# Second attention in runs of four and eight units, and gate inputs scaled once per event

## Reference

```python
x = _layernorm(x + _L0_attn_ref(x, ...))      # 16 heads of 8, decay by distance
x = _layernorm(x + _L0_ffn_ref(x, ...))       # one of 8 experts per token
x = _layernorm(x + _L1_attn_ref(x, ...))      # 16 heads of 64, below
x = _layernorm(x + _L1_ffn_ref(x, ...))       # 128 -> 512 -> 512 -> 512 -> 128
```

```python
q = _rmsnorm((x @ Wq).reshape(B, T, H, D), q_rms_w)
k = _rmsnorm((x @ Wk).reshape(B, T, H, D), k_rms_w)
v = (x @ Wv).reshape(B, T, H, D)
gate_logits = jnp.einsum('bthd,hd->bht', k, u_n) / math.sqrt(D)
gate = jax.nn.softplus(gate_logits)
bias = -dist[None, None] * omega_eff[None, :, None, None] * gate[:, :, None, :]
scores = jnp.einsum('bihd,bjhd->bhij', q, k) * scale + bias      # causal
y = jnp.einsum('bhij,bjhd->bihd', softmax(scores), v)
```

## Time and profile before

| | us |
|---|---|
| three runs | 2251.53, 2245.86, 2246.51 |
| median | 2246.51 |
| the profiled execution, its own time | 2246.59 |
| its span in the trace | 2244.8 |

### The profile page before, as it was taken

One profiled execution on the slowest core, in us unless ns is written; L12 is line 12 of the kernel. 1 busy time (PEld: TensorE's weight loads), 2 busy tenths in 40 slices (PEclk: granted clock), 3 DMA queues, 4 the chain that ended last, 5 costly groups with the idle time before them and its releaser, 6 DMA issues.

```text
span 2244.8 us, 34359 instructions
## 1 busy us (share of the span) xinstructions
PE 2050.4 (91%) x11728; PEld 1168.5 (52%) x11728; DVE 1368.2 (61%) x3345; ACT 1151.4 (51%) x1859; POOL 843.5 (38%) x544
## 2 busy tenths in 40 slices
PE   5799999998496888796999999999999999999998
PEld 2333333334395454453565656556665655655644
DVE  4788888884532878774666666666666654333311
ACT  2366666666353677673455555555555553223232
POOL 5000000001502345342677777777777773000000
PEclk8799999999598999995999999999999999999999
DMA  5233333113174779877577667776777687533300
GB/s 179 98 127 131 131 128 119 59 51 112 62 202 123 219 232 333 251 240 185 139 179 176 157 163 178 176 172 154 171 178 179 158 218 198 129 89 85 90 5 10
DMA packets 260300, 335.88 MB, mean 150 GB/s; under 512 B 22732, under 2 KB 181756, under 8 KB 259720
## 3 DMA queue, kind: packets, MB, share of 16 engines
q1 hardware_dynamic: 244824, 305.82, 50.6%
q0 software_dynamic: 7664, 24.39, 3.0%
q10 hardware_dynamic: 7640, 3.48, 0.5%
HBM read 193.69 MB, written 122.62 MB: 141 GB/s over the span
## 4 chain that ended last, share of the span: by engine, by line
PE 40%; issue 6%; DVE 4%; SPq 2%; DMA 1%; ACT 0%; DVEq 0%
PE ps L1287 10%; PE ps L956 6%; PE ps L940 6%; PE ps L909 6%; PE ps L941 5%; PE ps L1238 2%; DVE a1mx L1012 2%; PE ps L1298 1%; PE ps L1275 1%; PE ps L1276 1%; PE ps L943 1%; DVE a1mx L1008 1%; SPq L1162 1%; DMA a1FQ<-s_q 0%; DVE a1mx L1005 0%
## 5 line engine op out<-in xcount | busy, mean ns | idle before, releaser
L1123 POOL TENSOR_TENSOR a1sum<-a1sum,a1prob 128x1024 f32<-128x1024 f32 (+3 forms) x256 | 462.9, 1808 | 82.6 <-ACT a1prob L1066 50.5
L1066 ACT ACTIVATE a1prob<-ps 128x512 f32<-128x512 f32 (+2 forms) x640 | 328.0, 554 | 243.6 <-PE ps L943 211.9
L479 DVE TENSOR_REDUCE a0grid<-ps 128x8 f32<-128x1024 f32 x288 | 351.3, 1223 | 100.6 <-PE ps L351 63.1
L1005 DVE CUSTOM_DVE_ANT_0 ps<-ps,c_mask_ij 128x128 f32<-128x128 f32 x496 | 264.4, 551 | 193.9 <-issue 189.7
L580 ACT ACTIVATE a0prob<-ps 128x1024 f32<-128x1024 f32 x288 | 286.2, 1024 | 167.3 <-PE ps L377 110.5
L940 PE MATMUL ps<-a1QA,a1KA 69*128 69x512 f32 (+3 forms) x768 | 284.3, 378 | 4.6 <-DMA a1QA<-a1neg 4.6
L956 PE MATMUL ps<-a1prob,a1V 128*64 128x512 f32 (+3 forms) x1536 | 272.9, 498 | 3.9 <-ACT a1prob L1066 3.9
L941 PE MATMUL ps<-a1QB,a1KB 128*128 128x512 f32 (+3 forms) x768 | 263.1, 350 | 0.0
L909 PE MATMUL ps<-a1KA,a1QA 68*128 68x128 f32 x744 | 224.6, 381 | 4.3 <-DMA a1KA<-s_g 3.4
L956 PEld LDWEIGHTS ps<-a1prob,a1V 128*64 128x64 f32 x1536 | 102.7, 138 | 171.6 <-issue 138.1
L1008 DVE TENSOR_REDUCE a1mx<-ps 128x1 f32<-128x320 f32 x248 | 146.0, 589 | 70.1 <-PE ps L909 67.2
(11 more groups left out here) (267 smaller groups left out, 3163.1 us busy)
## 6 DMA issues: line engine op xcount, KB each, us to landing
a1FQ<-s_q SPq DMA_DIRECT2D x128, 256.0 KB, 7.9
a1KB<-s_k SPq DMA_DIRECT2D x128, 256.0 KB, 8.6
s_xs<-c_zero POOLq DMA_DIRECT2D x19, 1024.0 KB, 9.5
s_q<-mqkT SPq DMA_DIRECT2D x32, 512.0 KB, 4.4
s_v<-mv SPq DMA_DIRECT2D x32, 512.0 KB, 5.8
s_k<-a1KH SPq DMA_DIRECT2D x32, 512.0 KB, 4.9
s_k<-a1KL SPq DMA_DIRECT2D x32, 512.0 KB, 5.9
a1KA<-s_k SPq DMA_DIRECT2D x64, 256.0 KB
```

What stands on the lines that cost most here:

```text
L479: dve.tensor_reduce(grid[g % 2][:, :, a:b + 1:b - a], banks(("max", k)), axis=AX.X, op=ALU.max).then_inc(s1_free, 1)
L1005: dve.tensor_tensor_reduce(bank[:, 0:w], bank[:, 0:w], const["mask_ij"][:, BANK - w:BANK], 1.0, LOWEST, ALU.add, ALU.max, mx[:, x % 2, h, ...
L1066: act.activation(weights_of(g, u)[:, group[0]:group[-1] + 1, off:BANK], both(e, u, group), ACT.Exp).then_inc(weighed, 1)
L1123: pool.tensor_tensor(t[:, :, off:BANK], t[:, :, off:BANK], weights_of(g, u)[:, :, off:BANK], ALU.add).then_inc(summed, 1)
```

## The change

Four edits. The twelve units of a pair form two runs, 0 to 3 and 4 to 11, instead of three of four; the den job then stands after the scores of unit 11, ahead of the values of units 4 to 11. The turn job and the row's DMA go from unit 8 (9 in pair 0) to unit 11, and ACT's `keep_den` from unit 7 to unit 11. `store_den` of pair g-2 instead of g-1 is issued in SP's round of pair g, with the last two at the end. In the projection stage, the reciprocal of a K tile's norms goes to a buffer `kss` for all tiles, and the gate inputs are multiplied by it once per event, in `gates_a`, instead of once per tile.

```diff
--- before.py
+++ after.py
@@ -679,7 +679,8 @@
     units = [(c, j) for c in range(CH) for j in range((c + 1) * TILES)]
     NU = len(units)
     LAST = [TILES - 1, NU - 1]
-    runs = [range(r, r + TILES) for r in range(0, NU, TILES)]
+
+    runs = [range(0, TILES), range(TILES, NU)]
     width = [BANK - max(0, j * P - c * BANK) for c, j in units]
     pieces = [0]
     for w in width:
@@ -692,18 +693,17 @@
 
 
     share0 = ([0, 0, 2, 3, 3, 4, 4, 4, 4, 0, 0, 0], [0, 0, 0, 0, 0, 0, 0, 0, 0, 3, 3, 3])
-    turn_after = lambda g: TURN if g > 0 else TURN + 1
     assert sum(share0[0]) == NM and sum(share0[1]) == early
 
     def jobs(g, u):
 
         if g == 0:
             found = [("max", x, sum(share0[x - 1][:u]) + k) for x in (1, 2) for k in range(share0[x - 1][u])]
-            return [("turn", 1, 0)] + found if u == turn_after(0) else found
+            return [("turn", 1, 0)] + found if u == NU - 1 else found
         x = g + 2 if u >= TURN else g + 1
         first = sum(share[TURN:u]) if u >= TURN else early + sum(share[:u])
         found = [("max", x, first + k) for k in range(share[u])] if x < G else []
-        if u == TURN and g + 1 < G:
+        if u == NU - 1 and g + 1 < G:
             found.append(("turn", g + 1, 0))
         return found
 
@@ -880,7 +880,9 @@
                     load_y(2)
                     load_rec(2)
                     load_x(2)
-                if g > 0:
+                if g > 1:
+                    store_den(g - 2)
+                if g == G:
                     store_den(g - 1)
                 if g % PAIRS == 1 and g > 1 or g == G:
                     den_of_batch((g - 1) // PAIRS - (g < G))
@@ -1033,7 +1035,7 @@
                     for _ in jobs(g, u):
                         job(d)
                         d += 1
-                    if u == 2 * TILES - 1 and g > 0:
+                    if u == NU - 1 and g > 0:
                         d += 1
                 if g % PAIRS == 1 and g > 1:
                     invert(g // PAIRS - 1)
@@ -1092,10 +1094,10 @@
                         split(g + 2, (0, 3).index(u))
                     if u == TILES - 1:
                         keep(g, 0)
-                    if u == 2 * TILES - 1 and g > 0:
+                    if u == NU - 1 and g + 1 < G:
+                        row(g + 1)
+                    if u == NU - 1 and g > 0:
                         keep_den(g - 1)
-                    if u == turn_after(g) + 1 and g + 1 < G:
-                        row(g + 1)
                 keep(g, 1)
 
         def gpsimd_program():
@@ -1498,7 +1500,8 @@
         EVENTS = {24: range(0, 2), 72: range(2, 6), 96: range(6, 8)}
         wide = TILES * max(len(cs) for cs in EVENTS.values())
         zabs, g, gj = own("zabs", [P, wide, heads]), own("g", [P, wide, heads]), own("gj", [P, wide, heads])
-        z = own("z", [P, steps, TILES, heads])
+
+        z, kss = own("z", [P, steps, TILES, heads]), own("kss", [P, steps, TILES, heads])
         aug, augT = own("aug", [P, wide, P // heads, heads], F32R), [own(f"augT{r}", [4 * heads, CHUNK]) for r in range(2)]
         warm = own("warm", [P, 1])
         tmp = sq[0]
@@ -2234,17 +2237,15 @@
                 (tile, kind), i = kinds(n), nth(n)
                 c, t = divmod(tile, TILES)
                 dve.wait_ge(rooted3, i + 1)
-                dve.reciprocal(ss[i % 2][:, :], ss[i % 2][:, :]).then_inc(ss_full, 1)
+                norms = kss[:, c, t, :] if kind == WK else ss[i % 2][:, :]
+                dve.reciprocal(norms, ss[i % 2][:, :]).then_inc(ss_full, 1)
                 dve.wait_ge(ss_full, i + 1)
                 if i >= 3:
                     a = n // 3 * 3 + kind
                     old = [m for m in range(n) if kinds(m)[1] != WV][-3]
                     dve.wait_ge(t_full, at["half", old, 1] + 1)
-                if kind == WK:
-                    dve.wait_ge(z_full, c + 1)
-                    dve.tensor_tensor(z[:, c, t, :], z[:, c, t, :], ss[i % 2][:, :], ALU.mult).then_inc(z_scaled, 1)
                 dve.tensor_tensor(qk[i % 3][:, :].rearrange("p (h d) -> p h d", d=dim), pair(n).rearrange("p (h d) -> p h d", d=dim),
-                                  ss[i % 2][:, :].unsqueeze(2).to_broadcast([P, heads, dim]), ALU.mult).then_inc(scaled, 1)
+                                  norms.unsqueeze(2).to_broadcast([P, heads, dim]), ALU.mult).then_inc(scaled, 1)
 
             def parts(k):
 
@@ -2255,7 +2256,11 @@
             def gates_a(k):
 
                 n, zs, za, _, _ = parts(k)
-                dve.wait_ge(z_scaled, (events[k][-1] + 1) * TILES)
+                cs = events[k]
+                dve.wait_ge(z_full, cs[-1] + 1)
+                dve.wait_ge(ss_full, 2 * TILES * (cs[-1] + 1))
+                dve.tensor_tensor(zs, zs, kss[:, cs[0]:cs[-1] + 1, :, :].rearrange("p c t h -> p (c t) h"), ALU.mult).then_inc(z_scaled, 1)
+                dve.wait_ge(z_scaled, k + 1)
                 if k > 0:
                     dve.wait_ge(gated, GSTEP * k)
                 dve.scalar_tensor_tensor(za, zs, -1.0, zs, ALU.mult, ALU.max).then_inc(gated, 1)
```

## The result

The changed kernel takes 2409.64 us in the median of four runs (2402.62 to 2423.02), the kernel before 2249.02 beside it (2245.86 to 2252.29). The ratio is 1.072, with a 95% interval of 1.067 to 1.076: slower by about 161 us. The prediction was 2256, with a range of 2228 to 2286, and is wrong.

A forecast was written before the change was run, and what follows sets the result against it. The prediction took TensorE, busy 91% of the span, as the bound, with VectorE the other engine to watch. Its terms, -18 + 15 + 16 - 3 = +10 on 2246.59 us, gave 2256 us, range 2228 to 2286.

The forecast's parts named there:

- the walk: Second attention, one steady pair followed job by job: PE waits for VectorE's maxima from unit 8; pair 0.52 us longer.
- rival 4: Copy of queries' high half late for unit 8's first maximum: up to 3.9 us a pair, over 100 us; chance 0.07.
- Gates: Projection stage: multiplication of gate inputs taken out of the tiles removes PE's idle before K products; -18 us, ends -25 and -7.
- Two runs: Second attention: values no longer separate the maxima, so VectorE delays PE; 0.52 us a pair longer, +15 us over 29 pairs.
- The saved passage: Second attention: one passage from scores to values and back fewer per pair saves 0.4 us, ends 0.1 and 0.6.
- The clock: Second attention: PE's waits drop its clock in seven of 29 pairs, 2.3 us each; +16 us, ends 0 and 67.
- Turn and row: Transposition and row's DMA at unit 11 end the wait before the last pair; with passages of pairs 30 and 31, -3 us.
- The forecast's own case: Whole kernel: a few falls of PE's clock, 2246 to 2272 us; chance 0.43.
- Rival 2: Second attention: VectorE's join L1012 is not held, or VectorE catches up; sum -33, about 2213 us; chance 0.12.

The follow-up runs named there:

- e7: The changed kernel with 14 idle matmuls of 512 columns on PE ahead of its wait for the copy of the queries' high half; 2328.14 us, ratio 1.034.
- e1: The kernel before with the edit of the gate inputs alone; 2232.30 us, ratio 0.9927.
- e5: The changed kernel with the nine maximum jobs of units 8 to 11 reading other data, loaded long before, transfers unchanged; 2271.90 us, ratio 1.010.
- e8: The changed kernel with SyncE sending both copies of the queries' high half before the eight loads of 256 KB; 2274.43 us, ratio 1.011.
- e9: e8 with VectorE's join of row maxima as a one-operand reduction instead of a two-operand maximum; 2232.33 us, ratio 0.9893.
- e2: The changed kernel with three runs of four units again, its other edits kept; 2241.46 us, ratio 0.9962.
- e11: e9 with the copies of the high half issued ahead of the network's last loads and the store of the pair before; 2223.42 us, ratio 0.9841.
- e3: The changed kernel with ScalarE instead of SyncE issuing the copy of the queries' high half, right behind its split; 2374.06 us, ratio 1.0554.

## Why the prediction was wrong

**The step that failed** is the walk's at the first maximum of unit 8. The walk let PE wait there for VectorE alone, and the sum has no term for the copy of the queries' high half that this maximum reads: it stood at nothing. The prediction saw the wait, as rival 4: "If it took 8.6, PE would wait up to 3.9 us a pair, over 100 us in all; if about 3, nothing. A wait of 0.5 a pair gives 2271." The rival had the right transfer, the right instant and even the right duration (8.36 us, waits of 3.57), and I gave it 0.07, because "this one stays inside the chip". No row bore that out: in this kernel a copy inside SBUF took as long as the loads from outside, 8.4 us against 8.6, while all 16 DMA engines were taken. A window of 1201 to 1211 us shows a DMA share of 1.01 there and would have spoken against 3 us; the landing records gave 1.0 us of slack against a change that takes 4.6. The second mistake was in rival 4's price. It counted the waits only. The run of e7 puts them at 54 us, and the clock behind them at 85.

**The other terms of the sum** can be read in e1, e5 and e8, where the copy is in time.

- Gates: -18 on record, -16 in e1 (-21 to -12). Right, by the way described: idle before K from 19.7 to 1.1, Q's unchanged.
- Two runs: each pair was to be 0.52 us longer, 25.8 us, with a wait of about 0.7 at the fourth maximum and about 1.5 us of waits in all. Measured 25.75 against 25.27, a wait of 0.41, and 0.7 in all (25.70 - 25.03 in the window of e5). Right in length, and e9 shows that the held join is the reason; the waits were put too high.
- The saved passage: 0.4 us on record, with ends 0.1 and 0.6. With the join free, a pair of 24.93 us against 25.27 is 0.34.
- The clock: seven falls of 2.3 us, +16. Measured eight falls of 2.9, +23. Right in kind. The number seven is luck: it was picked between 0 and 29, as no row gave it. In e5 and e8 the falls come two or four pairs apart; why these pairs fall is not explained. By the rule of the Trainium skill, "TensorE: Matmul & The Clock Gate", section "A second HAM failure mode: psum-queue depth-cycling", short frequent idling makes the clock swing; here that held for eight pairs of 29 at waits of 0.4 us, not for nearly all.
- Turn and row: -3. The wait before the last pair fell from 2.29 us to 1.08 in the changed kernel, 0.35 in e5. Right in sign; smaller by about one. Without cover the row was to cost its 2 us each; with the values of four units as cover instead of eight it cost 0.3 us a pair in e2.

These add up to -16 + 14 + 23 - 2 = +19, and e5 measured +22 (+12 to +33). The forecast's own case (2246 to 2272) held, at its upper edge, for the kernel it described, a changed kernel whose copy comes in time. Rival 2, the faster one at 2213, was given little for the right reason (L1014 stayed at 1.42 us). e11, with the join free and SyncE's order changed twice, is 36 us under before, against the -33 on record. The nearness is in part luck: the gates' 16 and the pairs' 11 (747.6 against 758.3 us from pair 1 to pair 31) make 27 of it, and the rest I can't place.

## What to carry to other kernels

When work is moved earlier, list each transfer that it reads and take from the trace not how long such a transfer should need but when this one landed, how full the DMA engines were up to then, and how much slack is left; a change of order that uses up more than the slack turns it into a wait in every round. Price such a wait together with the clock behind it: here the clock cost more than the waits. And when an order is made tighter, send what is wanted first ahead of bulk loads that have slack; a copy on another engine's queue did not get past them.

## What was not expected of the hardware

- The same transfer of 256 KB inside SBUF took 8.4 us from issue to use behind large loads on its own queue, and 9.3 us from a separate queue (ScalarE's), at a DMA share near 1 in both kernels. Sent ahead of the large loads (e8) it landed 4.2 us after its issue.
- Waits of PE of 1.8 us in pairs of 30.7 us went with a mean granted clock of 0.84 (e3), the same as waits of 3.5 us (0.84). Identical waits of 0.42 us were followed by a fall to the 1.2 GHz level in eight pairs of 29 and by none in the others (e5); in e8 it was eight of 29 too. What tells those pairs apart stays open. e7 shows the waits to be the cause of the larger loss: with work in place of the wait, the clock was 0.99.
- A join of eight values that takes 170 ns as a one-operand reduction took 1420 ns as a two-operand maximum beside GpSimd's adds (166 ns where none ran), and through a chain of maxima in three PSUM places this decided between pairs of 24.9 us and pairs of 25.75 with falls of the clock.
